# Attention layer: reciprocals by a round trip through memory, a leaky activation shared by ScalarE and GpSimd, transposes ahead of the mixing burst

## The reference, cut to what matters

```
def gat_layer(x, graph, W, b):
    h = x @ W
    s = jnp.einsum('bnd,bmd->bnm', h, h) * graph
    s = jnp.where(s == 0.0, NEG_INF, s)
    a = jax.nn.softmax(s, axis=2)
    return jnp.einsum('bnm,bmd->bnd', a, h) + b
heads = jax.vmap(lambda W, b: gat_layer(flow_x, graph, W, b))(Wh, bh)
...
x = jax.nn.leaky_relu(cat, negative_slope=0.01)
out = gat_layer(x, graph, W_out, b_out)
```

## Time and profile before

| | |
|---|---|
| median of the 3 runs shown | 3390.31 us (3386.8 to 3392.65) |
| profiled execution | 3389.07 us |
| its span (first to last instruction) | 3387.3 us |
| mean granted TensorE clock | 0.975 of full speed |
| busy over the span | TensorE 91%, VectorE 88%, ScalarE 68%, GpSimd 25% |

### The profile page before, as it was taken

One profiled execution on the slowest core, in us unless ns is written; L12 is line 12 of the kernel. 1 busy time (PEld: TensorE's weight loads), 2 busy tenths in 40 slices (PEclk: granted clock), 3 DMA queues, 4 the chain that ended last, 5 costly groups with the idle time before them and its releaser, 6 DMA issues. The chain is left out here.

```text
span 3387.3 us, 48344 instructions
## 1 busy us (share of the span) xinstructions
PE 3089.4 (91%) x15547; PEld 1885.1 (56%) x15547; DVE 2982.4 (88%) x3851; ACT 2300.4 (68%) x3525; POOL 830.0 (25%) x580
## 2 busy tenths in 40 slices
PE   7998899999999999999999999799598888888857
PEld 3676566666666666666666666599554333333323
DVE  3578999999999999999999999688756999999944
ACT  0122677777777777777777777677346999999831
POOL 0123000000000000000000000000114999999921
PEclk9999999999999999999999999899799999999978
DMA  4000000000000000000000000000000000000001
GB/s 97 0 1 1 1 1 0 0 0 0 0 0 0 0 0 0 0 0 0 0 0 0 0 0 0 1 1 0 9 0 1 1 1 1 1 1 1 1 2 25
DMA packets 30364, 12.16 MB, mean 4 GB/s; under 512 B 27984, under 2 KB 29264, under 8 KB 30288
## 3 DMA queue, kind: packets, MB, share of 16 engines
q1 hardware_dynamic: 25056, 10.04, 1.3%
q10 hardware_dynamic: 5232, 1.12, 0.2%
HBM read 9.06 MB, written 2.10 MB: 3 GB/s over the span
## 5 line engine op out<-in xcount | busy, mean ns | idle before, releaser
L660 ACT ACTIVATE hid_work<-hid_work,hid_nmax 128x1024 f32<-128x1024 f32 x512 | 589.5, 1151 | 305.5 <-DVE hid_nmax L644 305.5
L632 DVE TENSOR_TENSOR hid_work<-hid_score_ps,A 128x1024 f32<-128x1024 f32 x512 | 618.3, 1208 | 30.0 <-PE hid_score_ps L593 29.9
L644 DVE CUSTOM_DVE_ANT_0 hid_work<-hid_masks,hid_work 128x1024 f32<-128x1024 f32 x512 | 620.6, 1212 | 0.2 <-DVE hid_masks L652 0.2
L1690 POOL TENSOR_TENSOR el<-el,node_edge 128x1024 f32<-128x1024 f32 x256 | 610.5, 2385 | 17.8 <-DVE el L1672 11.5
L671 ACT COPY hid_probsT<-hid_turn_ps 128x512 f32<-128x512 f32 x1024 | 542.2, 580 | 101.9 <-PE hid_turn_ps L607 101.9
L607 PEld LDWEIGHTS hid_turn_ps<-ident,hid_work 128*128 128x128 f32 x4096 | 458.4, 141 | 249.3 <-issue 206.0
L607 PE MATMUL hid_turn_ps<-ident,hid_work 128*128 128x128 f32 x4096 | 544.9, 276 | 4.9 <-ACT hid_probsT L671 3.9
L818 PE MATMUL hid_mix_ps<-hid_probsT,x_now 128*64 128x512 f32 x2048 | 497.2, 606 | 33.4 <-DVE hid_Zn L892 30.5
L592 PE MATMUL hid_score_ps<-hid_SX,hid_Y 128*128 (+1 forms) x1024 | 476.9, 466 | 2.6 <-DVE hid_SX L993 2.6
L593 PE MATMUL hid_score_ps<-hid_SX,hid_Yl 128*128 (+1 forms) x1024 | 405.5, 396 | 0.0
L1643 PE MATMUL spread<-hT_parts,pick 128*128 128x512 f32 x1024 | 309.2, 425 | 65.9 <-DVE u_buf L1666 61.6
(11 more groups left out here) (280 smaller groups left out, 4080.2 us busy)
## 6 DMA issues: line engine op xcount, KB each, us to landing
A<-in_adj_dram SPq DMA_DIRECT2D x4, 1024.0 KB, 9.8
X<-in_x_dram SPq DMA_DIRECT2D x8, 256.0 KB, 8.8
out_dram<-X SPq DMA_DIRECT2D x8, 256.0 KB, 3.4
wa<-in_L_gnn_weight_dram ACTq DMA_DIRECT2D x2, 256.0 KB, 15.2
wb<-in_L_gnn_weight_dram ACTq DMA_DIRECT2D x2, 256.0 KB, 13.6
wh<-in_L_gnn_Wh_dram SPq DMA_DIRECT2D x2, 256.0 KB, 5.5
incid<-in_L_gnn_H_dram SPq DMA_DIRECT2D x2, 256.0 KB, 3.5
wo<-in_L_gnn_W_out_dram SPq DMA_DIRECT2D x1, 256.0 KB, 6.1
```

Of the source, the lines that this page charges most:

```text
L632: nc.vector.tensor_tensor(work[:, kk % 4, :], score_ps[kk % 2][:], A[:, kk % NT, :], ALU.mult).then_inc(s["weighted"], 1)
L644: nc.vector.tensor_tensor_reduce(work[:, kk % 4, :], masks[:, kk % 2, :], work[:, kk % 4, :], -1.0, 3.0e38, ALU.add, ALU.min, nmax[:, kk % ...
L660: nc.scalar.activation(work[:, kk % 4, :], work[:, kk % 4, :], ACT.Exp, bias=nmax[:, kk % 4:kk % 4 + 1], scale=-1.0, accum_out=rowsum[:, k ...
L1690: nc.gpsimd.tensor_tensor(el[:, q % ELS, :], el[:, q % ELS, :], coefT[:, q // C, :], ALU.mult).then_inc(s_weighted, 1)
```

## The change

- R is gone from `EARLY`. The SP queue gets a program (`sp_body`): for each group it stores the four reciprocals of every row (128 x 4) to a tensor in device memory, `r_rows`, contiguously, and when that has landed loads the 512 numbers back as a broadcast to all 128 partitions of `rbc`. The load also waits until the previous group's Zn is made. The numbers now lie in the order (q a) in `rbc`: `vec_norm` reads them with a step of four elements, and waits for the load's semaphore instead of for ScalarE's copy. `vec_invert` waits for the store of two groups ago.
- The leaky activation leaves VectorE. With z the product plus bias, ScalarE writes 0.01 z into a new tile `sloped` (the bias, held in `bh`, is multiplied by 0.01 once), then at the end of the step `act_relu` writes 99 relu(0.01 z) into `leaky`, and GpSimd adds the two (`pool_leaky`), four times an item.
- In odd steps `pe_turn` now comes before `pe_burst`, and the burst's parts are of six and two matmuls.
- An unused semaphore of a later layer is dropped from its list.

```
-            EARLY = {0: ("R", 8), 2: ("W", 14), 4: ("R", 8), 6: ("W", 14), 8: ("R", 8), 10: ("W", 14), 12: ("R", 8),
-                     14: ("W", 14)}
+            EARLY = {2: ("W", 14), 6: ("W", 14), 10: ("W", 14), 14: ("W", 14)}
...
-                for mt in range(4 * part, 4 * part + 4):
+                for mt in range(6) if part == 0 else range(6, NT):
...
+                nc.scalar.activation(sloped[:, half, :], misc_ps[:], ACT.Identity, bias=bh_now[:],
+                                     scale=SLOPE).then_inc(misc_read, 1)
...
+            def act_relu(act, i, k, first, last):
+                if not present(k, False, first, last):
+                    return
+                g, u, half, _ = group_of(i, k, EARLY[k][1])
+                act.wait_ge(misc_read, use(i, k, False, first, last) + 1)
+                act.nop(nofuse=True)
+                nc.scalar.activation(leaky[:, u, half, :], sloped[:, half, :], ACT.Relu,
+                                     scale=1.0 / SLOPE - 1.0).then_inc(relu_made, 1)
...
-                nc.vector.scalar_tensor_tensor(out=part, in0=part, scalar=0.01, in1=part, op0=ALU.mult,
-                                               op1=ALU.max).then_inc(leaky_made, 1)
+            def pool_leaky(pool, i, k, first=False, last=False):
+                _, u, half, _ = group_of(i, k, EARLY[k][1])
+                part = leaky[:, u, half, :]
+                pool.wait_ge(relu_made, 1 if first else 4 * i - 2 + k // 4)
+                pool.nop(nofuse=True)
+                nc.gpsimd.tensor_tensor(part, part, sloped[:, half, :], ALU.add).then_inc(leaky_made, 1)
...
+                if not first:
+                    vec.wait_ge(r_stored, 64 * i + 16 * ((k - 6) // GROUP) - 32)
+                    vec.nop(nofuse=True)
                 nc.vector.reciprocal(at.rinv[:, slots], at.rowsum[:, slots]).then_inc(s["inverted"], 1)
...
-                vec.wait_ge(misc_read, use(i, k - 2, False, first, last) + 1)
+                vec.wait_ge(r_loaded, 64 * i + 16 * ((k - 10) // GROUP + 1))
                 vec.nop(nofuse=True)
-                nc.vector.tensor_tensor(Zn[:, half, :], mix_ps[:], rbc[:], ALU.mult).then_inc(s["normed"], 1)
+                nc.vector.tensor_tensor(Zn[:, half, :].rearrange("p (a q) -> p a q", a=GROUP),
+                                        mix_ps[:].rearrange("p (a q) -> p a q", a=GROUP),
+                                        rbc[:].rearrange("p (q a) -> p a q", a=GROUP), ALU.mult).then_inc(s["normed"], 1)
...
+                at.pe_turn(pe, i, k, first, last)
                 pe_burst(pe, i, k, first, last)
-                at.pe_turn(pe, i, k, first, last)
...
+            def sp_body(sp, i, first=False):
+                for d in range(4):
+                    sp.wait_ge(s["inverted"], 4 * i + d + 1)
+                    sp.nop(nofuse=True)
+                    sp.dma_start(r_rows[d], at.rinv[:, d * GROUP:(d + 1) * GROUP]).then_inc(r_stored, 16)
+                    if not first or d >= 1:
+                        sp.wait_ge(s["normed"], 4 * i + d)
+                        sp.nop(nofuse=True)
+                    sp.wait_ge(r_stored, 64 * i + 16 * (d + 1))
+                    sp.nop(nofuse=True)
+                    sp.dma_start(rbc[:], r_rows[d].rearrange("q a -> (q a)").unsqueeze(0).to_broadcast([P, HALF])
+                                 ).then_inc(r_loaded, 16)
+                    sp.wait_ge(r_loaded, 64 * i + 16 * (d + 1))
+                    sp.nop(nofuse=True)
```

More of the change, by code:

```diff
@@ L545, in adjacency_stack_kernel @@
         MASKED = -1.0e16
+        SLOPE = 0.01
         BODY = 2 * NT
@@ L710, in adjacency_stack_kernel @@
             rbc = sb("hid_rbc", [P, HALF], F32, scope)
+            r_rows = nc.dram_tensor("hid_r_rows", [4, P, GROUP], F32).ap()
+            r_stored, r_loaded = sem("hid_r_stored"), sem("hid_r_loaded")
             Zn = sb("hid_Zn", [P, 2, HALF], F32, scope)
             leaky = sb("leaky", [P, 2, 2, HALF], F32, scope)
+            sloped = sb("sloped", [P, 2, HALF], F32, scope)
+            relu_made = sem("hid_relu_made")
             mix_ps, misc_ps = at.mix_ps, ps("hid_misc_ps", [P, HALF], scope)
@@ L765, in pe_early @@
                 g, u, half, ib = group_of(i, k, EARLY[k][1])
[L766 to L778, removed]
+                if u == 0 and half == 0:
+                    pe.wait_ge(staged_w, ib + 1)
+                pe.wait_ge(s["normed"], g + 1)
+                pe.nop(nofuse=True)
+                done = nc.tensor.matmul(misc_ps[:], wh_now[:], Zn[:, half, :], start=True, stop=True)
                 done.then_inc(misc_made, 1)
@@ L830, in act_early @@
                 act.wait_ge(misc_made, n + 1)
[L831 to L838, removed]
+                if k == 6 and not first:
+                    act.wait_ge(leaky_made, 4 * i - 3)
+                    act.nop(nofuse=True)
[6 more added lines that the diff above has]
+                act.wait_ge(misc_read, use(i, k, False, first, last) + 1)
+                act.nop(nofuse=True)
+                nc.scalar.activation(leaky[:, u, half, :], sloped[:, half, :], ACT.Relu,
+                                     scale=1.0 / SLOPE - 1.0).then_inc(relu_made, 1)
             def act_late(act, i, k, first, last):
@@ L863, in vec_late @@
                     nc.vector.tensor_tensor(acc, acc, misc_ps[:].unsqueeze(1), ALU.add).then_inc(misc_read, 1)
-            def vec_leaky(vec, i, k, first, last):
-                if not present(k, False, first, last) or EARLY[k][0] != "W":
-                    return
+            def pool_leaky(pool, i, k, first=False, last=False):
                 _, u, half, _ = group_of(i, k, EARLY[k][1])
                 part = leaky[:, u, half, :]
-                vec.wait_ge(misc_read, use(i, k, False, first, last) + 1)
-                nc.vector.scalar_tensor_tensor(out=part, in0=part, scalar=0.01, in1=part, op0=ALU.mult,
-                                               op1=ALU.max).then_inc(leaky_made, 1)
+                pool.wait_ge(relu_made, 1 if first else 4 * i - 2 + k // 4)
+                pool.nop(nofuse=True)
+                nc.gpsimd.tensor_tensor(part, part, sloped[:, half, :], ALU.add).then_inc(leaky_made, 1)
             def vec_invert(vec, i, k, first, last):
@@ L906, in act_step @@
                 at.act_copy(act, i, k, first, last)
+                act_relu(act, i, k, first, last)
             def vec_step(vec, i, k, first=False, last=False):
@@ L910, in vec_step @@
                 vec_norm(vec, i, k, first, last)
-                if k:
-                    vec_leaky(vec, i, k - 1, first, last)
                 at.vec_shift(vec, i, k, first, last)
@@ L939, in pool_body @@
                 if not first:
+                    pool_leaky(pool, i, 2)
                     pool.wait_ge(s["mixed"], 4 * i)
@@ L946, in pool_body @@
                 if not first:
+                    pool_leaky(pool, i, 6)
+                    pool_leaky(pool, i, 10)
                     pool.wait_ge(misc_read, use(i, 10, False, first, False) + 1)
@@ L952, in pool_body @@
                 stage_x(pool, bass.ds((i + 1) // HEADS % J, 1), 0)
+                pool_leaky(pool, i, 14, first)
                 if not first:
@@ L962, in adjacency_stack_kernel, with _ @@
             block = scope.enter_context(nc.Block())
+            @block.sync
+            def _(sp):
+                sp_body(sp, 0, first=True)
+                with sp.Fori(1, ITEMS) as i:
+                    sp_body(sp, i)
             @block.gpsimd
@@ L967, in _ @@
                 stage_x(pool, bass.ds(0, 1), 0)
+                nc.gpsimd.tensor_scalar(bh[:], bh[:], SLOPE, None, ALU.mult).then_inc(cleared, 1)
+                pool.wait_ge(cleared, 1)
                 nc.gpsimd.memset(h2T[:], 0.0).then_inc(cleared, 1)
@@ L971, in _ @@
                     pool_body(pool, i)
+                for k in (2, 6, 10):
+                    pool_leaky(pool, ITEMS, k, last=True)
             @block.scalar
@@ L1003, in _ @@
                     x_lo(b)
-                vec.wait_ge(cleared, 1)
+                vec.wait_ge(cleared, 2)
                 bodies(vec, vec_step, ITEMS)
@@ L1317, in adjacency_stack_kernel @@
             wide = [ps(f"l2b_wide{k}", [P, N], scope) for k in range(3)]
-            (s_made, s_copied, s_turned, s_turn_copied, s_agg, s_exped, s_gn, s_gexp, v_steps, s_h, s_he, s_he_c, s_fc,
+            (s_made, s_copied, s_turned, s_turn_copied, s_agg, s_exped, s_gn, s_gexp, v_steps, s_he, s_he_c, s_fc,
              s_tanh, s_se, s_elu, s_ct, s_ct_copied, s_cexp, s_ht) = (
                 sem(f"l2b_{n}") for n in ("scored", "score_copied", "turned", "turn_copied", "agg_made", "exped",
-                                          "gn_made", "gate_exped", "vector_steps", "incid_turned", "he_turned",
+                                          "gn_made", "gate_exped", "vector_steps", "he_turned",
                                           "he_copied", "fc_made", "tanhed", "se_made", "elu_exped", "coef_turned",
```

## The result

The changed kernel takes 3465.36 us (median of 4 runs, 3455.9 to 3471.57) against 3388.56 us, a ratio of 1.0224, 95% interval 1.0192 to 1.0257: slower by 77 us. The profiled execution of the changed kernel took 3471.57 us (span 3469.8), 82.5 us more than that of before.

What follows compares the result with a forecast made beforehand. VectorE and TensorE were both nearly full, and VectorE would set the time: 52.40+2.2+4.5 = 59.1 us an item against 55.66, +3.44 times 32 = +110 us, so 3500 us. Range 3350 to 3535.

Steps and rivals of the forecast that it cites:

- both prices: On VectorE in the hidden layer: strided Zn read +2.2 us and additions holding up masks +4.5 us an item.
- the likeliest reading: Strided read and held-up masks both cost VectorE: 3500 us, own range 3465 to 3535, chance 0.52.
- VectorE sets the time in full once it has more than 0.86 us more to do: Hidden layer: VectorE's only gap an item is 0.86 us, before a weighing; work added beyond it counts in full.
- The leaky step frees 2.40 us an item: VectorE loses four leaky steps of 0.60 us an item, so its work falls from 54.80 to 52.40 us.
- The strided read: VectorE's Zn reads reciprocals with a 16-byte step: 0.55 us more each, four an item, +2.2 us.
- The additions stand before the mask: GpSimd's addition arrives during VectorE's shift and goes ahead of the zero mask: 1.13 us each, +4.5 us an item.
- Sum: VectorE's item in the hidden layer: 52.40+2.2+4.5 = 59.1 us against 55.66, times 32 = +110 us.
- TensorE's 53.25: TensorE's item without its 0.97 us wait and the reciprocal transposes' 1.44 us: 55.66-0.97-1.44 = 53.25 us.
- Round trip hidden: Reciprocals' store and load take 7.7 us, at worst 11.2, covered by 11.03 us before Zn: costs nothing.
- The order and the parts at nothing: TensorE's changed order priced at nothing, within 0.1 us per odd step; parts of six and two add no matmuls.
- the one on the other side: Rival: additions cost VectorE nothing, the strided step costs; 54.6 us an item, -1.06, 3356 us, chance 0.15.

Runs made afterwards that it cites:

- e1: Changed kernel with Zn's multiplication reading rbc contiguously, so reciprocals of the wrong columns are used: 3423.65 us, ratio 1.0106 to the kernel before.
- e2: Changed kernel with GpSimd adding only 4 of the 512 columns: 3349.01 us, ratio 0.9882 to the kernel before.
- e8: Changed kernel with the leaky activation back on VectorE, without relu on ScalarE or addition on GpSimd: 3411.69 us, ratio 1.0069 to the kernel before.
- e5: Changed kernel with GpSimd's addition also waiting until VectorE has made the same step's zero mask: 3353.57 us, ratio 0.9895 to the kernel before.
- e3: Changed kernel with GpSimd adding only 4 columns and Zn reading rbc contiguously: 3318.5 us, ratio 0.9794 to the kernel before.
- e6: Changed kernel with the store writing reciprocals in order a, q (512 pieces of 4 bytes) and Zn reading contiguously: 3705.01 us, ratio 1.0936 to the kernel before.
- e4: Kernel before with only TensorE's order changed, transposes in front of the burst and parts of six and two: 3374.39 us, ratio 0.9948.
- e9: Changed kernel with the addition after the mask and ScalarE reordering the loaded reciprocals so Zn reads contiguously: 3335.02 us, ratio 0.9844 to the kernel before.
- e10: The e9 kernel with TensorE's old order, burst before transposes and parts of four and four: 3375.59 us, ratio 0.9958 to the kernel before.

## Why the prediction was right

It forecast slower, 3500 us, and 3465 came, 77 us over the kernel before where 110 were forecast. The mechanism was the right one, with both prices. The range of 3350 to 3535 took in faster kernels too, so that 3465 lies in it says little; of the narrower 3465 to 3535 given to the likeliest reading it is the very edge, and two of the four runs lie below it.

- *VectorE sets the time in full once it has more than 0.86 us more to do*: shown. It has no gap, and e1, e2, e8 move with its sum.
- *The leaky step frees 2.40 us an item*: agrees with e8 within the sum; no run takes the leaky step away by itself.
- *The strided read*: its price was mis-sized. Taken 0.55 us each from L419 (bounds 0 and 0.61), measured 0.39 start to start, so 1.56 us an item and not 2.2: 20 us of the 33 that are missing (77 for 110). This is the term that was most wrong. Another 6 us are the additions' price and 8 the masks that went free. The rule of the Trainium skill ("Advanced Engine Details and Errata", Memory Cachelines) has its direction right: 16 bytes of step already cost. Its size is not that of L419, where both streams had the step and the time doubled.
- *The additions stand before the mask*: shown by the mask's 1.76 us, by e2 and e5. The place was worked out as D+2.45 to 2.55 and is D+2.38. The price, taken as 1.13 us (by its own figures 1.31-0.15 = 1.16), is 1.08 (1.68 of the mask, less 0.60). It holds in 100 of 107 steps. The Trainium skill ("SBUF — State Buffer", Who interferes with whom) says that whoever issues first gets the shared pair. The prediction put this as who starts first, and by the letter of that the mask would have won. If an operation that waits counts as issued, the trace agrees in those 100 steps: the addition's record starts at 1212.13, the mask's at 1213.02. The seven others go against it.
- *Sum*: 52.40+1.56+4.32 = 58.28, and 58.28 is what an item with all four masks held takes. The mean of 26 items is 58.02, 2.37 over before; times 32 that is 76 us, for 77 between the medians and 82.5 between the two profiled executions.
- *TensorE's 53.25*: 53.36 in e3. *Round trip hidden*: yes, 1.4+4.1 us in about 10: the load issued at 1216.98 lands about 1221.1, and the Zn that needs it starts at 1225.13. The spare 4 us don't bear a store 6.7 us longer, as e6 shows. *The order and the parts at nothing*: wrong in general, 16 us in e4 and 41 us in e9 against e10, of which 18 are the parts. In the changed kernel, where VectorE has no gap, I take it for right; no run puts the old order there.

Of the rivals, the one on the other side (additions for nothing) is what e5 makes true by moving them: 3353.57 us, where the rival's sum gave 3356. That the two are so near is luck: the rival's 54.6 has the step at 2.2 us. With 1.56 the sum is 53.96; e5's item takes 54.31 and has again a shift behind an addition (0.18 us) and a short gap before a weighing (0.15).

## What to carry to other kernels

Work given to GpSimd was nearly free here beside instructions of VectorE that read a PSUM operand (e5), and cost 1.08 us of VectorE beside the shift and the mask. Look at what VectorE runs when the GpSimd operation becomes ready. If it is an operation with both operands in SBUF (the shift) or a TENSOR_SCALAR in SBUF (the mask), make GpSimd wait until those are past; one added wait was worth 112 us here. Price a change of layout on the engine that reads it, and give the reordering to an engine with time to spare. Two engines within 2% of each other hide each other's savings, as e4 (16 us) and e9 against e10 (41 us) show for the same edit, so test an edit on either also with the other one relieved. And one item of a trace is not the mean: compare the same instruction over all items before trusting a sum to the hundredth.

## What the runs showed of the hardware that was not expected

- Between the shift and the mask, a GpSimd addition that has been waiting is served in 100 of 107 steps (109 of 109 in e1), though the mask is recorded as started 0.06 us before the shift ends. In the seven others the mask is served first (0.68 to 0.76 us) and the addition takes 2.70 to 2.79 us. After an addition the mask seems to be served ahead of GpSimd's next copy (0.70 us for one of 0.24).
- A step of 16 bytes in one of two operands costs VectorE 0.39 us for 512 columns (1.09 us, not 0.68). ScalarE's copy with such a read takes 1.15 us, not some 0.6.
- A store of 2 KB from 128 partitions to device memory lands in 1.4 us in pieces of 16 bytes and in 8.1 us in pieces of 4 (e6).
